# Attention by L1 distance: a ring row of four keys by half the features, and one joined row in every second tile

## The reference, cut to what matters

```python
# h: tokens mixed by 8 rounds of a recurrence, [8, 750, 64];  x = layernorm(h)
v = (x @ wqv_w.T + wqv_b).reshape(b, t, 24, 64)
q, vf, vb = v[:, :, :8], v[:, :, 8:16], v[:, :, 16:]
k = x[:, :, None, :] * wk[None, None]                 # 8 heads
a[b, s, t, h] = -sum_w |q[b,s,h,w] - k[b,t,h,w]| / 8   # every pair of tokens, w = 0..63
a = softmax over s, with one extra row of zeros
o = sum over heads of  a @ vf + a^T @ vb
h = h + x + (o * sigmoid(1.702 * o)) @ fanin_w.T + fanin_b
h = h + a mixture of 8 experts, the best 2 of each token (64 -> 256 -> 64)
```

## Time and profile before

| | |
|---|---|
| median of three runs | 8665.07 us |
| the profiled execution | 8663.45 us |
| span of its trace | 8661.6 us |
| PE, ACT, DVE busy in the span | 99%, 89%, 83% |
| `phase_tokens` | 0 to about 286 us |
| `phase_attend` | about 286 to 8408 us |
| `phase_feed` | about 8408 us to the end |
| mean granted clock of TensorE | 0.993 |

### The profile page before, as it was taken

How to read it: one execution, slowest core, us unless ns; L and a number is a source line. 1 busy time by engine, 2 the same in 40 slices (tenths; PEclk the granted TensorE clock), 3 DMA queues, 4 the chain that set the end, 5 groups by cost and what they waited for, 6 DMA issues and landing times. The chain is left out here.

```text
span 8661.6 us, 247366 instructions
## 1 busy us (share of the span) xinstructions
PE 8539.5 (99%) x110998; PEld 6073.1 (70%) x110998; DVE 7231.5 (83%) x5701; ACT 7722.2 (89%) x3712; POOL 42.5 (0%) x35
## 2 busy tenths in 40 slices
PE   8899999999999999999999999999999999999999
PEld 3477775568755896669955688558966888557983
DVE  4688888888888888888888888888888888888874
ACT  2699999999999999999999999999999999999976
POOL 1000000000000000000000000000000000000000
PEclk9899999999999999999999999999999999999999
DMA  4200000000000000000000000000000000000000
GB/s 134 76 17 2 17 2 17 2 2 17 2 17 2 17 2 2 17 2 17 2 17 2 2 17 2 17 2 17 2 2 17 2 17 2 17 2 2 2 12 8
DMA packets 135369, 114.17 MB, mean 13 GB/s; under 512 B 111464, under 2 KB 114984, under 8 KB 134040
## 3 DMA queue, kind: packets, MB, share of 16 engines
q1 hardware_dynamic: 121611, 78.50, 4.0%
q10 hardware_dynamic: 12692, 19.51, 0.7%
HBM read 57.75 MB, written 40.22 MB: 11 GB/s over the span
## 5 line engine op out<-in xcount | busy, mean ns | idle before, releaser
L794 PE MATMUL sc<-ring,window 128*32 128x375 f32 x96000 | 7919.5, 478 | 23.4 <-DVE ring L913 15.2
L845 ACT ACTIVATE ring<-qx,xs 128x3000 f32<-128x3000 f32 x2624 | 7176.3, 2791 | 620.2 <-PE sc L794 619.0
L913 DVE TENSOR_SCALAR ring<-qx,xs 128x3000 f32<-128x3000 f32 x3376 | 6131.6, 1837 | 1048.5 <-PE sc L794 988.9
L794 PEld LDWEIGHTS sc<-ring,window 128*32 128x32 f32 x96000 | 5455.4, 109 | 2101.6 <-issue 763.2
L761 PEld LDWEIGHTS acc<-ext,vf 128*32 128x32 f32 x9408 | 383.2, 109 | 50.1 <-issue 15.3
L748 PE MATMUL acc<-ex,vb 128*32 128x375 f32 x3088 | 415.9, 477 | 1.5 <-DVE ex L878 1.5
L863 DVE COPY sc<-kept 128x750 f32<-128x750 f32 x385 | 362.4, 941 | 64.2 <-ACT ex L830 53.5
L761 PE MATMUL acc<-ext,vf 128*32 128x128 f32 (+1 forms) x9408 | 401.7, 270 | 0.2 <-DVE ext L889 0.2
L889 DVE STREAM_TRANSPOSE ext<-ex 128x768 f32<-128x768 f32 x385 | 374.4, 972 | 0.6
L830 ACT ACTIVATE ex<-sc 128x750 f32<-128x750 f32 x385 | 297.7, 773 | 5.6 <-PE sc L794 5.6
L748 PEld LDWEIGHTS acc<-ex,vb 128*32 128x32 f32 x3088 | 201.5, 108 | 70.1 <-issue 25.4
(11 more groups left out here) (161 smaller groups left out, 783.3 us busy)
## 6 DMA issues: line engine op xcount, KB each, us to landing
qx<-scratch_qk SPq DMA_DIRECT2D x60, 375.0 KB
scratch_v<-ext SPq DMA_DIRECT2D x21, 960.0 KB, 7.9
scratch_qk<-qx ACTq DMA_DIRECT2D x32, 375.0 KB, 6.5
vb<-scratch_v SPq DMA_DIRECT2D x120, 92.0 KB
vf<-scratch_v SPq DMA_DIRECT2D x120, 88.0 KB
scratch_v<-ext ACTq DMA_DIRECT2D x4, 960.0 KB, 7.1
xs<-scratch_x SPq DMA_DIRECT2D x15, 187.5 KB
vb<-scratch_v SPq DMA_DIRECT2D x120, 1.8 KB
```

Of the source, the lines that this page charges most:

```text
L794: mm = pe.matmul(bank[32 * j:32 * j + 32, h, 0:HALF], window[:, HALF_NH * g + j, ROWS - 1 - i:3 * ROWS - 1 - i], ring[:, slot, j, h * HALF ...
L845: act.activation(flat(ring[:, (HALF * g + k) % RING, :, :]), flat(qx[g][:, :, :]), ACT.Abs, bias=xs[g][:, 1, k:k + 1], scale=0.5).then_inc ...
L913: vec.tensor_scalar(flat(ring[:, (HALF * g + k) % RING, :, :]), flat(qx[g][:, :, :]), xs[g][:, 0, k:k + 1], xs[g][:, 1, k:k + 1], ALU.max, ...
```

## The change

The key range is cut in four instead of two: a step now has partition 32 a + w for key c + 188 a (a = 0 to 3) and feature w of one *half* of the features (`part` 0 low, 1 high). So a group of four keys (a *quad*) takes two steps, its low half and its high half, with the same `window` columns but weights of their own. A tile is still 32 keys, now 8 quads, and the last one is 4 quads.

In every second tile (`merged(t)`, t odd, the last one among them) the first quad's two steps become one. DVE makes it in `both`: for each of the four heads it writes `max(q_low, k_low) * ratio` into the slot (L952, 128 x 750 each; ratio is low weight over high weight), waits until these are written, and adds `max(q_high, k_high)` over the whole slot (L955, 128 x 3000, the slot is an input as well). PE sums the slot with the high weights. The half of the key that a DVE step subtracts is missing in such a row; it comes back through the bank's preset, which in merged tiles adds a number per partition (`kx`; PE makes its sums in `sums`, DVE copies them in `key_sums`). A pair has 188 x 2 - 12 = 364 steps instead of 375.

The doubled `qx` (low and high half side by side) takes SBUF: the ring has five slots. `hx` goes to DRAM at the end of `phase_tokens` and comes back at the start of `phase_feed`; `ksum` has one buffer. The loads of a pair are 69 DMAs instead of 38. Slots are numbered anew in each pair, so at a pair's start one slot is passed over (`TURN` = 365).

```diff
-ROWS = 16
+QUADS = 8
+QUARTER = HALF - HALF // 2
+PART = D // 2
-RING = 6
+RING = 5
-NLOADS = 2 + 4 + 4 * HALF_NH + 4 * HALF_NH
+NLOADS = 1 + 4 + 16 + 8 * HALF_NH + 4 * HALF_NH
+def merged(t):
+    return t % 2 == 1
+def steps(t):
+    one = [(0, 2)] if merged(t) else [(0, 0), (0, 1)]
+    return one + [(i, part) for i in range(1, quads(t)) for part in range(2)]
+STEPS = first_step(NT)
+TURN = -(-STEPS // RING) * RING
...
+            for h in range(2):
+                for a in range(2):
+                    p0 = 32 * (2 * h + a)
+                    queue.dma_start(self.xs[g][p0:p0 + 32, 0, :, 0:QUARTER - a],
...
+            for part_w in range(2):
+                for dup in range(4):
+                    for k in range(2):
+                        queue.dma_start(self.qx[g][32 * dup:32 * dup + 32, part_w, k:HALF_NH:2, :],
...
                     sp.wait_ge(x_made, NQC)
+                    sp.wait_ge(h_made, 1)
+                    sp.dma_start(scratch_h, hx).then_inc(at.h_stored, 16)
...
-        EXP_AT, FILL_AT, Z_AT, RZ_AT, A_AT, EXT_AT, KEEP_AT = 6, 8, 9, 10, 12, 14, 15
+        EXP_AT, FILL_AT, Z_AT, RZ_AT, A_AT, EXT_AT, KEEP_AT = 6, 8, 8, 9, 10, 12, 14
...
+                    for j in range(HALF_NH):
+                        for part in range(2):
+                            mm = pe.matmul(kept[32 * j:32 * j + 32, 0, KX:KX + NT],
+                                           window[:, part, HALF_NH * g + j, QUADS - 1:QUADS + 31],
+                                           xs[g][:, 0, part, 0:QUARTER:QUADS], start=(part == 0), stop=(part == 1),
...
-                        mm.then_inc(ring_free, 1)
+                        mm.then_inc(ring_free, 1 if t < NT - 1 or i < rows(t) - 1 else 1 + TURN - STEPS)
...
+                def key_sums(pairs, g):
+                    vec.wait_ge(sums_made, pairs)
+                    vec.tensor_scalar(kx[:, g, :], kept[:, 0, KX:KX + NT], -0.5, None, ALU.mult).then_inc(kx_made, 1)
+                def fill(pairs, g, t, done):
+                    par = t % 2
+                    vec.wait_ge(kx_made, pairs)
+                    vec.wait_ge(ex_made, done)
+                    if merged(t):
+                        vec.tensor_scalar(sc[par][:, :, 0:HALF], kept[:, :, 0:HALF], kx[:, g, t:t + 1], None,
+                                          ALU.add).then_inc(bank_set, 1)
+                    else:
+                        vec.tensor_copy(sc[par][:, :, 0:HALF], kept[:, :, 0:HALF]).then_inc(bank_set, 1)
+                def both(n, g, t):
+                    slot = first_step(t) % RING
+                    c = QUADS * t
+                    for j in range(HALF_NH):
+                        vec.tensor_scalar(ring[:, slot, j, :], qx[g][:, 0, j, :], xs[g][:, 0, 0, c:c + 1],
+                                          ratio[:, HALF_NH * g + j:HALF_NH * g + j + 1], ALU.max, ALU.mult).then_inc(low_made, 1)
+                    vec.wait_ge(low_made, n * (HALF_NH * NM) + HALF_NH * (merges_before(t) + 1))
+                    vec.scalar_tensor_tensor(flat(ring[:, slot, :, :]), flat(qx[g][:, 1, :, :]), xs[g][:, 0, 1, c:c + 1],
+                                             flat(ring[:, slot, :, :]), ALU.max, ALU.add).then_inc(made_vec, 1)
...
+                sp.dma_start(hx[:, :], scratch_h).then_inc(h_in, 16)
...
                 vec.wait_ge(w_first, 48)
+                vec.wait_ge(h_in, 16)
                 added(0)
```

More of the change, by code:

```diff
@@ L102, in load_part @@
             for h in range(2):
[L103 to L109, removed]
+                for a in range(2):
+                    row = b * HALF + h * TC + QUARTER * a
+                    p0 = 32 * j + QUADS * (2 * h + a)
+                    queue.dma_start(self.vb[g][p0:p0 + QUADS, 0:NT - 1, :],
+                                    scratch_v[bass.ds(row, QUADS * (NT - 1)), cols]
+                                    .rearrange("(t p) d -> p t d", p=QUADS)).then_inc(into, 16)
+                    queue.dma_start(self.vb[g][p0:p0 + LQUADS - a, NT - 1, :],
+                                    scratch_v[bass.ds(row + QUADS * (NT - 1), LQUADS - a), cols]).then_inc(into, 16)
         else:
@@ L547, in _ @@
                     pool.wait_ge(part, 5)
[L548 removed]
+                    pool.tensor_tensor(hx, ht[:, :], xt, ALU.add).then_inc(h_made, 1)
                 @block.scalar
@@ L694, in phase_attend, with merges_before @@
         NPAIR = 2 * B
-        NA = made_before(HALF, True)
-        NV = HALF - NA
-        EXP_AT, FILL_AT, Z_AT, RZ_AT, A_AT, EXT_AT, KEEP_AT = 6, 8, 9, 10, 12, 14, 15
+        NA = made_before(NT - 1, STEPS, True)
+        NV = STEPS - NA
+        NM = sum(merged(t) for t in range(NT))
+        KX = 400
+        EXP_AT, FILL_AT, Z_AT, RZ_AT, A_AT, EXT_AT, KEEP_AT = 6, 8, 8, 9, 10, 12, 14
         BACK_AT, FORWARD_AT = 2, 5
         def rows(t):
-            return LROWS if t == NT - 1 else ROWS
+            return len(steps(t))
+        def merges_before(t):
+            return sum(merged(u) for u in range(t))
         def due(place, i, t):
@@ L886, in turn @@
                             vec.wait_ge(at.v_stored[k], 16 * len(range(k, NVC, NVS)))
+                    if t == NT - 1 and g == 1:
+                        vec.wait_ge(at.h_stored, 16)
                     if t % GROUP == 0:
@@ L1435, in arrange @@
     for p in range(128):
-        if not on_scalar(p % ROWS):
-            select[3 * (p // 32):3 * (p // 32) + 3, p] = -0.5
+        for part in range(2):
+            if not on_scalar(p % QUADS, part):
+                lo = 3 * (HALF_NH * part + p // 32)
+                select[lo:lo + 3, p] = -0.5
     avg, fant, pick = np.zeros((128, 128), f), np.zeros((128, 128), f), np.zeros((128, NE, 128), f)
```

222 lines of the change are left out of this document (126 added, 96 removed).

## The result

| | before | after |
|---|---|---|
| median of 17 runs | 8665.12 us (8659.83 to 8668.92) | 8681.99 us (8678.38 to 8687.59) |
| the profiled execution | 8663.45 us | 8680.59 us |
| span of its trace | 8661.6 us | 8678.8 us |
| granted clock over the span | 0.99 | 0.99 |

The ratio after over before is 1.0020, with a 95% interval of 1.0014 to 1.0027: 16.9 us slower. The forecast was 8679 us. Its total is off by 3 us, but two of its terms were off by more and one was missing, as the traces show.

What follows compares the result with a forecast made beforehand. PE was taken to bound the attention stage; -14 us there, +24 for the first pair's loads, +2 first preset and +3 last stage gave 8678, forecast as 8679 us (own range 8650 to 8705; 8 in 10: 8618 to 8725).

Steps and rivals of the forecast that it cites:

- The bound and the joined row: Attention stage: PE sets the time; 11 fewer steps a pair save 222 us; DVE's joined row takes 5.80 us.
- The wait: First step of every merged tile: PE stands still 1.14 us for the joined row, leaving -14 us over 16 pairs.
- the link ahead of it: From the end of PE's step k - 5 to DVE's start on the joined row in the freed slot: 0.35 us.
- The last tile: Last tile of a pair: `sums` covers 0.65 us of PE's wait, which leaves 0.49 us.
- The returns: Returns of the attention loop: no term; PE's 1.1 us waits were not to touch its clock, the stage's rest covered.
- The start: First pair's loads, issued by ACT ahead of the attention stage: +24 us (9 to 46).
- The first preset: Start of the attention stage: the first preset stands behind its own sums, +2 us.
- The last stage: L1299 needs `hx`, which is issued fourth and lands later: +3 us (2 to 5).
- the short row: Rival, faster: joined row of 5.50 us gives 8623 us, at 5.27 us 8579; chance 0.24 (0.05 of it at 5.27).
- the slow pieces: Rival, slower: DVE's pieces at one number a cycle, joined row 6.90 us, 8891 us in all; chance 0.05.
- a late DVE: Rival, slower: DVE comes late to the joined row 192 times; 0.2 us are 38 us, 8717 us; chance 0.09.
- The issue path: Rival, slower: first pair's issues on ACT's queue cost +46 us instead of +24, 8701 us; chance 0.12.

Runs made afterwards that it cites:

- the last experiment: Kernel with back and forward moved and two batches a turn, now without the first pair's sixteen small `vb` loads (L152): 8490.91 us in a single run.

## Why the prediction was right or wrong

**The bound and the joined row: right.** That PE sets the stage, that 222 us go, and that one wait of about a microsecond per merged tile eats them is what the trace shows, 192 times. The joined row took 5.79 us for 5.80. The two estimates it rests on, a pointer's 60 ns and 1.044 ns a number with two tensors, held at 668 and 3344 ns. By the Trainium skill, "Vector Engine (DVE) Microarchitecture Reference", section "Measured stream behaviour on trn2" (about 75 ns an instruction beyond its numbers once they queue), it would have been 5.27 us; the trace, with 5.79 us, disagrees.

**The wait: right mechanism, 0.08 us too long.** 1.06 for 1.14. The joined row's own time is exact to 0.02. The fault is in the link ahead of it, which came from another place: step k - 5 ends at 2889.99 + 6 x 1.263 = 2897.57, and the pieces start at 2897.84, 0.27 us later for the forecast's 0.35. Behind it PE starts 0.06 us after the row's end, for 0.04. Over 11 tiles of 16 pairs that is 14 us.

**The last tile: too cheap.** 0.74 us for 0.49, 4 us in all. The wrong term is the 0.65 us that `sums` was to cover, a fourth of its eight records' lengths. The records overlap more than fourfold: in the kernel before, the interval with `sums` is 21.83 us and the same one without 21.46, so `sums` cost 0.37 us and could cover no more. 1.06 less 0.37 is 0.69, near the 0.74. The small matmuls did fall into the wait, as forecast; behind them PE still waited:

```profile
3331.30 0.38 PE L843 MATMUL kept<-xs,window 128*32 128x24 f32 x16
3332.00 4.00 PE L865 MATMUL sc<-ring,window 128*32 128x375 f32 x48 [0.32 <-DVE ring L955]
```

With 0.1 us won at the borders this gives, to about 1 us, the measured 24 for 14.

**The returns: a step that was missing.** "That PE stands still for 1.1 us twice in 86 us should not touch its clock" is right where it was said of, and "the rest of that stage is covered" is not: I read a border without a return and the clock at the one with a return, and never the price of that return, though the pair that ends in one takes 508.7 us and its neighbour 505.3. A place that costs 3.4 us without any work in it is a place that a change of the code around it may move. It went to 6.8, and the sum by 23 us. Two signs of the forecast failed with it: the pair period is 506.9 us ((7905.6 - 302.2) / 15), not 506.0, and the clock is lower at the returns.

**The start: right path, 24 for 16.5.** Against the measured rows (start us, length us of the issues):

```profile
218.26 0.36 ACTq L126 DMA_DIRECT2D ksum<-scratch_ks  x1
...
218.65 1.80 ACTq L131 DMA_DIRECT2D xs<-scratch_x  x4
220.48 7.65 ACTq L138 DMA_DIRECT2D qx<-scratch_qk  x16
...
236.33 2.97 ACTq L149 DMA_DIRECT2D vb<-scratch_v  x1
...
290.35 2.03 ACTq L160 DMA_DIRECT2D vf<-scratch_v  x1
```

`qx` 7.65 us for 2.67 (+5, forecast 6), `xs` 1.80 (+1.4, forecast 1), `vb` 26.2 for 19.3 (+7, forecast 11), `ksum` 2.8 earlier (forecast 3 later), and 4.7 more from the last issue to its landing (forecast 3). These shift by a few us with no change to the loads: the kernel before with five slots began its stage 3.4 us earlier than before did. `vb` was too dear because I priced issues one by one; the last experiment shows that the number of issues does not set the time. What does was not separated: `qx`, ahead of `vb` in the queue, now moves 16 x 187.5 KB, twice what it did, and that was in no term of the forecast.

**The first preset: nothing for +2.** Behind the start of the stage it came as early as before: the first `back` follows after 9.73 us, for 9.97.

**The last stage: right.** `hx` is waited for 5.34 us, and the stage is 1.9 us longer, where 3 was forecast (2 to 5).

```profile
8431.94 0.74 DVE L1406 SCALAR_TENSOR_TENSOR h<-px_d,fbc,hx 128x500 f32<-128x500 f32 x1 [5.34 <-DMA hx<-scratch_h]
```

The rivals: the short row is refuted (668 ns a piece), as are the slow pieces of 6.90 us in all and a late DVE (PE's wait is the same where DVE had nothing to spare). The issue path was dear, but below its forecast. The 3 us between forecast and result are luck: errors of -10, +23, -2.5, -7.5 and -1 left so little.

**What stays open.** Why PE halts a second time behind a return, and why so early and long in after (2.84 us behind one record) and in its versions, is not known. It is not the ring's size, nor the number of merged rows. What all the versions with the dear return share is the rest of the change, the new code of the steps and of `sums` among it; which part of it matters was not tested. That the engines fetch code behind the jump would fit halts that nothing releases, but no run here shows it.

## What to carry to other kernels

A shared buffer row must be made in (slots - 1) steps of its consumer less the links. Work that is joined to save steps makes one row long, so compare that one row with the slack, not the engine's mean load; a wait there can be paid by moving the consumer's other work between the step that frees the slot and the step that needs it, which adds no work and brought 161 us here. Take a period across the return of a hardware loop apart from the others before summing, and try more turns in its body. Do not price loads on a busy queue one by one: leaving out sixteen issues whose own lengths added up to 14 us brought 3.

## What the runs showed of the hardware

- A return of the loop cost DVE 2.2 us of issue and PE two halts, 3.4 us in all in one kernel and 6.8 us in another. Behind two halts of 2.11 and 2.84 us with one record between, the granted clock of 8 us was 0.79 and PE's weight loads came at half their rate for 2.9 us; behind a single wait of 2.8 to 3.1 us (the kernel before with five slots) it was 0.79 at five returns and 1.00 at two. One wait of about 1 us in 43 left it at 1.00.
- Single issues on ACT's queue lasted 0.30 to 2.97 us in after; sixteen of them took 11.8 us among 32, and 23.0 us when the other sixteen were left out.
- A preset of 750 numbers took DVE 1000 ns with a pointer to a scalar and 941 ns without one, 59 ns less; at 500 numbers two instructions of the kernel before differ by 60 ns.
